# Attention scores on groups of array rows, and the causal mask of the exponentials moved from TensorE to a GpSimd select

## The reference, cut to what matters

```python
# layer 1: 16 heads, each split into two halves of 4 channels (32 half-heads), causal
def _causal_attn(q, k, v, scale, mask):
    s = jnp.einsum('bhqd,bhkd->bhqk', q, k) * scale
    s = jnp.where(mask, s, jnp.finfo(s.dtype).min)
    p = jax.nn.softmax(s, axis=-1)
    return jnp.einsum('bhqk,bhkd->bhqd', p, v)
mask = jnp.tril(jnp.ones((seqlen, seqlen), dtype=bool))[None, None]
a1 = _causal_attn(q1, k1, v1, scale, mask)
a2 = _causal_attn(q2, k2, v2, scale, mask)
y = jnp.concatenate([a1 - lp * a2, a1 + lp * a2], axis=-1)

# layer 2: 16 heads of 8 channels, no mask
scores = jnp.einsum('bhqd,bhkd->bhqk', Q, K) / np.sqrt(Hd).astype(jnp.float32)
attn = jax.nn.softmax(scores, axis=-1)
out = jnp.einsum('bhqk,bhkd->bhqd', attn, V)
```

## Time and profile before

| | kernel before |
|---|---|
| median of 3 runs | 1531.0 us (1527.28 to 1532.28) |
| profiled execution | 1529.98 us |
| its span on the core | 1528.2 us |
| mean granted TensorE clock | 0.899 |
| PE (TensorE matmul) busy | 1342.3 us, 88% of the span |
| PEld (TensorE weight load) busy | 812.0 us, 53% |
| DVE (VectorE) busy | 970.2 us, 63% |
| ACT (ScalarE) busy | 665.5 us, 44% |
| POOL (GpSimd) busy | 203.0 us, 13% |

### The profile page before, as it was taken

One profiled execution on the slowest core, in us unless ns is written; L12 is line 12 of the kernel. 1 busy time (PEld: TensorE's weight loads), 2 busy tenths in 40 slices (PEclk: granted clock), 3 DMA queues, 4 the chain that ended last, 5 costly groups with the idle time before them and its releaser, 6 DMA issues.

```text
span 1528.2 us, 23814 instructions
## 1 busy us (share of the span) xinstructions
PE 1342.3 (88%) x9318; PEld 812.0 (53%) x9334; DVE 970.2 (63%) x2093; ACT 665.5 (44%) x1424; POOL 203.0 (13%) x189
## 2 busy tenths in 40 slices
PE   7977788998897787888989989999779899999999
PEld 4455657876765674343756656654334323234565
DVE  3568743343453677876877876465667888876365
ACT  2444143753541431023433435666446566666621
POOL 1132170000202300035000000044100100000000
PEclk8988698998996987569999999999989999999988
DMA  8000123341000310015253363211212303000000
GB/s 248 6 1 1 29 67 100 98 113 49 27 1 14 70 22 3 0 41 146 89 130 109 107 168 120 92 45 29 64 20 53 64 5 66 3 1 28 1 8 21
DMA packets 65100, 86.22 MB, mean 56 GB/s; under 512 B 9566, under 2 KB 49374, under 8 KB 63326
## 3 DMA queue, kind: packets, MB, share of 16 engines
q1 hardware_dynamic: 60892, 76.30, 19.1%
q0 software_dynamic: 4096, 8.40, 2.0%
HBM read 62.19 MB, written 22.48 MB: 55 GB/s over the span
## 4 chain that ended last, share of the span: by engine, by line
PE 64%; DVE 14%; DMA 8%; ACT 4%; issue 4%; POOL 3%; SPq 2%; DVEq 0%; ACTq 0%
PE psA L404 32%; PE psB L404 25%; PE psB L408 5%; DVE mx L1485 3%; POOL slots_x L1922 2%; PE psA L408 2%; ACT pbuf L1738 2%; DMA wA<-slots_x 2%; POOL tH L1935 1%; DVE st L1168 1%; ACT pbuf L1820 1%; DMA arena<-scr1k 1%; DMA scr1k<-arena 1%; DMA arena<-slots_x 1%; DMA arena<-scr2k 1%
## 5 line engine op out<-in xcount | busy, mean ns | idle before, releaser
L1820 ACT ACTIVATE pbuf<-psA 128x512 f32<-128x512 f32 (+3 forms) x768 | 350.0, 489 | 250.2 <-PE psA L404 243.1
L1485 DVE TENSOR_REDUCE mx<-psA 128x1 f32<-128x512 f32 (+3 forms) x608 | 377.7, 657 | 101.2 <-PE psA L404 97.2
L404 PE MATMUL psA<-arena 64*64 64x128 f32 (+9 forms) x1632 | 243.2, 308 | 14.0 <-DVE mx L1485 11.1
L404 PEld LDWEIGHTS psA<-arena 64*64 64x64 f32 (+3 forms) x1632 | 131.5, 138 | 115.2 <-DVE mx L1485 44.2
L1738 ACT ACTIVATE pbuf<-psA,st,rq 128x128 f32<-128x128 f32 x256 | 92.7, 467 | 112.8 <-DVE st L1172 112.8
L404 PE MATMUL psA<-arena,w 96*128 96x512 bf16 (+4 forms) x320 | 114.8, 411 | 19.3 <-DMA arena<-scr2k 10.4
L404 PE MATMUL psA<-w_identb,w_mdiagT 128*128 128x128 bf16 x512 | 110.9, 243 | 0.0
L404 PE MATMUL psA<-w_mdiagT,w_identb 128*128 128x128 bf16 x512 | 110.0, 223 | 0.0
L404 PE MATMUL psB<-xf,wA 128*128 128x128 f32 x624 | 93.8, 295 | 6.1 <-DMA wA<-in_moe 5.7
L404 PE MATMUL psB<-pbuf,arena 128*5 128x512 f32 (+3 forms) x1024 | 95.3, 445 | 0.4 <-ACT pbuf L1820 0.4
L1935 POOL DMA_INDIRECT tH<-slots_y,slot_i x64 | 62.0, 968 | 237.7 <-DMA slots_y<-tH 219.3
(11 more groups left out here) (295 smaller groups left out, 2136.2 us busy)
## 6 DMA issues: line engine op xcount, KB each, us to landing
wA<-in_moe SPq DMA_DIRECT2D x39, 576.0 KB, 3.8
wA<-in_moe SPq DMA_DIRECT2D x39, 256.0 KB, 3.0
slots_x<-wA SPq DMA_DIRECT2D x20, 256.0 KB, 3.7
slots_y<-tH SPq DMA_DIRECT2D x18, 256.0 KB, 3.6
wA<-slots_x SPq DMA_DIRECT2D x15, 256.0 KB, 4.1
arena<-scr2k SPq DMA_DIRECT2D x48, 64.0 KB
scr1q<-arena SPq DMA_DIRECT2D x4, 384.0 KB, 4.0
scr1k<-arena SPq DMA_DIRECT2D x4, 384.0 KB, 4.1
```

The lines of the kernel that those rows point to most:

```text
L404: return pe.matmul(out, lhsT, rhs, start=start, stop=stop, skip_group_check=True)
L1485: dv.tensor_reduce(m[:, t, h:h + c], topb("mx", lay, b, n)[:, 0:c * k].rearrange("p (c k) -> p c k", c=c), AX.X, ALU.max) \
L1820: ac.activation(pb(lay, b, s, j)[:, 0:T - q0_], scoreb("ex", lay, b, s, j)[:, 0:T - q0_], ACT.Exp, bias=0.0, scale=1.0) \
```

## The change

1. **Row groups.** Each half-head of layer 1 gets its own group of 32 rows (24, with the maxima 27), four groups side by side. Each head of layer 2 gets 64 rows (48, with the maxima 51), two groups. A score matmul reads the rows of its own group alone. Keys are no longer block-diagonal, so `HK` shrinks to a quarter in layer 1 and a half in layer 2. New functions `q_of` and `k_of` give the rows. The maxima passes go through the heads with the row group changing from unit to unit, and `ex` visits the four tiles of a group in the order `HO`.
2. **The mask of `mx`** opens each unit as one matmul over all its diagonal blocks (352 matmuls over 128, 256 or 512 columns in place of 512 over 128), and the scores are added to it.
3. **The mask of `ex`** is gone from TensorE. GpSimd's `affine_select` writes zero above the diagonal into the first 128 columns of four finished tiles at once (128 of them, 128x4x128), and `pv` of layer 1 waits for it (`ex_masked`) in place of the exponential.
4. **The ring `pb`** has twelve tiles in place of eight. The four new ones lie in `arena`.
5. **`pv`, `tail` and the projections** form a stream of their own, `k` in `MERGE`, in place of a fixed place in the main stream. `MERGE` has new contents throughout.
6. **The transfers.** Stacking takes 48 loads of 4 rows per batch in layer 1 (9 of 16, 32 or 48 rows before) and 24 loads of 8 rows in layer 2 (18 of 8 or 16 rows before). The maxima come in by 4 loads in layer 1 and 2 in layer 2 (1 before). The rows of ones are set by a GpSimd memset of the whole of `HK` in place of a transfer from `in_kone`.

The diff, cut to its core:

```diff
 MERGE = (
-    "11ab2ab7c2b2c2bc2bcbcbc3bcb4cb4cb3cb2cbc2b2c2bcbcj4cj2cb2c2jb2j4c3j4cbjcjc2jbjc2j2cb2cjcj2cj8c3j5cjc"
+    "11a3ba3ba9c3bc2bc2bcb4cb2cb2cb2cb5cbcbc2b2cb4cjcj2cjcb3c2j6c2jbjcjcjbc2jcj2cbcj2cj6c2jcjcjb3j4cj2cb2"
...
-        pb = Ring(ptiles)
+        pb = Ring(ptiles + [arena[:, 7680 + T * k:8192 + T * k] for k in range(4)])
+        pfour = [pbuf[:, 2 * k:2 * k + 2, :, 0:P].rearrange("p a b c -> p (a b) c") for k in range(2)]
+        pfour.append(arena[:, 7680:9728].rearrange("p (k c) -> p k c", k=4)[:, :, 0:P])
...
+        HS = {1: 32, 2: 64}
+        HO = {1: (0, 1, 2, 3), 2: (0, 2, 1, 3)}
...
+        def q_of(lay, i, h, rows):
+            p = HS[lay] * (h // 8)
+            return HQ[lay][i][p:p + 6 * HD[lay] + rows, h % 8, :]
...
-                for h, t, o in tops_of(lay)[n]:
-                    k = (t + 1) * P if CAUSAL[lay] else T
-                    m = mm(bank[:, o:o + k], HQ[lay][i][0:96, h % 8, t * P:(t + 1) * P], HK[lay][i][0:96, kof(lay, h), 0:k],
-                           True, not CAUSAL[lay])
-                    if CAUSAL[lay]:
-                        m = mm(bank[:, o + k - P:o + k], mdiagT, identb, False, True)
+                if CAUSAL[lay]:
+                    mm(bank[:, 0:c * k].rearrange("p (c k) -> p c k", c=c)[:, :, k - P:k], mdiagT,
+                       identb.unsqueeze(1).to_broadcast([P, c, P]), True, False)
+                for h, t, o in part:
+                    m = mm(bank[:, o:o + k], q_of(lay, i, h, 0)[:, t * P:(t + 1) * P], k_of(lay, i, h, 0)[:, 0:k], not CAUSAL[lay], True)
...
-                m = mm(bank[:, 0:T - q0_], HK[lay][i][0:HR[lay], kof(lay, g), kb * P:(kb + 1) * P],
-                       HQ[lay][i][0:HR[lay], g % 8, q0_:T], True, not causal)
-                if causal:
-                    m = mm(bank[:, 0:P], identb, mdiagT, False, True)
-                m.then_inc(*ex_mm.up(lay, b, s, j))
+                mm(bank[:, 0:T - q0_], k_of(lay, i, g, 3)[:, kb * P:(kb + 1) * P], q_of(lay, i, g, 3)[:, q0_:T], True, True) \
+                    .then_inc(*ex_mm.up(lay, b, s, j))
...
-                pe.wait_ge(*ex_p.at(lay, b, s, 3))
+                pe.wait_ge(*(ex_masked.at(b, s) if CAUSAL[lay] else ex_p.at(lay, b, s, 3)))
...
+            def ex(lay, b, s, j):
+                if CAUSAL[lay] and j == 3:
+                    v = pfour[pb.turns[lay, b, s, 0] % len(pb.aps) // 4]
+                    po.wait_ge(*ex_p.at(lay, b, s, 3))
+                    po.affine_select(v, v, [[0, 4], [1, P]], ALU.is_ge, fill=0.0, base=0, channel_multiplier=-1).then_inc(*ex_masked.up(b, s))
...
+                for j in range(P // HS[lay]):
+                    r, rows = HS[lay] * j, slice(HS[lay] * j, HS[lay] * j + HS[lay])
+                    for part, n in ((0, 3), (1, 2), (2, 1)):
+                        qs = dr["q"][b][part, rows].rearrange("(i g) c -> i g c", g=8)
                         for k in range(n):
-                            for j in range(2):
...
+                            sy.dma_start(HQ[lay][i][r:r + D], qs).then_inc(*stack_in[b].up(lay))
+                            ks = dr["k"][b][k, rows].rearrange("(i g) c -> i g c", g=8)
+                            if lay == 1:
+                                ks = ks.rearrange("i (h r) c -> i h r c", h=2)[:, :, j, :]
+                            sy.dma_start(HK[lay][i][r:r + D], ks).then_inc(*stack_in[b].up(lay))
+                            r += D
```

More of the change, by code:

```diff
@@ L32 @@
[L32 to L36, removed]
@@ L279, in build, with k_of @@
                      for k, r in (("q", P), ("k", P), ("m", HG[lay]))} for lay in HB}
-        def kof(lay, h):
-            return h % 8 // 4 * 4 + h // 8 if lay == 1 else h
+        def q_of(lay, i, h, rows):
+            p = HS[lay] * (h // 8)
+            return HQ[lay][i][p:p + 6 * HD[lay] + rows, h % 8, :]
+        def k_of(lay, i, h, rows):
+            p = HS[lay] * (h // 8)
+            return HK[lay][i][p:p + 6 * HD[lay] + rows, h % 8 // 4 if lay == 1 else h % 8, :]
         def tile_of(lay, n):
@@ L369, in build @@
         l3_in = signals("weights3_loaded", 1, 16)
-        kone_in = [signals(f"key_ones_loaded{i}", 1, 16) for i in range(NBUF)]
         part_q = [signals(f"q_parts_stored{b}", 1, 16) for b in range(NB)]
@@ L1901, in clr @@
             def clr(lay, b):
-                if lay == 2:
+                if lay == 1:
+                    for t in range(4):
+                        po.wait_ge(*ln_xc.at("h2", t))
+                    po.wait_ge(*bo_done.at(3))
+                    if b:
+                        po.wait_ge(*wo_mm.at(3, 1))
+                        po.wait_ge(*kn_turned.at(3, 3))
+                else:
                     po.wait_ge(*pv_mm.at(1, b + 1, 31))
-                    if b == 0:
-                        po.wait_ge(*pv_mm.at(1, 2, 31))
-                    po.memset(HK[2][b].rearrange("p g c -> p (g c)").bitcast(F32), 0.0).then_inc(*kz_done.up(b))
+                po.memset(HK[lay][b].rearrange("p g c -> p (g c)").bitcast(F32), ONE2).then_inc(*kz_done.up(lay, b))
             def rot(b, n):
@@ L2047, in mxT @@
                 sy.wait_ge(*part_m[b].at(lay))
-                sy.dma_start(HQ[lay][i][96:HR[lay], :, :], dr["m"][b].rearrange("s (j g) c -> (s j) g c", g=8)) \
-                    .then_inc(*max_in[b].up(lay))
+                for j in range(P // HS[lay]):
+                    r = HS[lay] * j + 6 * HD[lay]
+                    sy.dma_start(HQ[lay][i][r:r + 3], dr["m"][b][:, 8 * j:8 * j + 8, :]).then_inc(*max_in[b].up(lay))
             def wi3_():
@@ L2066, in store @@
                     sy.nop()
[L2068 removed]
+            return dict(init=init, xl=xl, wl=wl, st=stored, w2=w2, stack=stack, mxT=mxT, wi3=wi3_, w3=w3, store=store)
         def streams():
@@ L2110, in streams @@
                 main += [("kn0", b, kv) for kv in range(4)] + [("v0", b, j) for j in range(4)] + [("sc", b, i) for i in range(8)]
+            take = []
             for lay in (1, 2):
@@ L2159, in streams @@
                         mix += [("yv", b, i - 1, x)] * (0 < i < 9) + [("tp", b, i, x)] * (i < 8)
-            return [norm, main, ffn, stack, top] + flows + [mix]
+            return [norm, main, ffn, stack, top] + flows + [mix, take]
         def merged():
@@ L2168, in merged @@
                 else:
-                    order += [next(todo["abcdefghij".index(c)]) for _ in range(int(n or 1))]
+                    order += [next(todo["abcdefghijk".index(c)]) for _ in range(int(n or 1))]
                     n = ""
@@ L2265, in constants @@
     c["selq1"], c["selk1"] = c["selq1"].astype(np.float32), c["selk1"].astype(np.float32)
-    one = np.zeros((3, 4, 8, T), np.float32)
-    for h in range(8):
-        one[:, h % 4, h] = 1
-    c["kone1"] = bf(one.reshape(12, 8, T))
-    one = np.zeros((3, 2, 16, T), np.float32)
-    for h in range(16):
-        one[:, h // 8, h] = 1
-    c["kone2"] = bf(one.reshape(6, 16, T))
     c["hsel"] = (i[:, None] // 8 == np.arange(16)[None]).astype(np.float32)
```

133 lines of the change are left out of this document (53 added, 80 removed).

## The result

The changed kernel took 1725.52 us (median of 4 runs, 1719.77 to 1731.78) against 1529.14 us for the kernel before in the same session (4 runs). The ratio is 1.129, with a 95% interval of 1.124 to 1.134. The forecast was 1523 us with a range of 1485 to 1568. It was wrong in size and in sign.

A forecast was written before the change was run, and what follows sets the result against it. TensorE was taken to bound both attentions, taking turns with DVE in the first maxima. Terms +6 +3 -16 -18 +8 +9 = -8 on 1530.0 gave 1522, 1523 as a median, range 1485 to 1568.

The forecast's parts named there:

- Stacks, +8 forecast: Stacked-row loads at batch starts: more, smaller loads change each batch's wait, together +8 us, bounds -24 and +35.
- the second rival: Few-row loads not covered at batch starts: each causal batch starts 9 us late, 35 in place of 8, so 1550; chance 0.22.
- `pv` later and ring of twelve, -18 forecast: Both attentions: later pv ties TensorE and ScalarE less closely, saving a quarter of 78.2 us of waits, bounds 0 and -35.
- the first rival: Later pv gives nothing, as the score waits for its own bank, and the stacks are hidden: 1533; chance 0.20.
- Second attention, -16 forecast: Second attention, 1201 to 1393 us: -40 of overlap, +11 of steps; -16 us taken, bounds -29 and +11.
- First maxima, +6 forecast: First batch's maxima, 588 to 676 us: 88 units at 0.90 us take 79 where they took 73, +6 us.
- the bound that I gave for a gain: First batch's maxima: -12 us if the granted clock rises above 0.55.
- -27 - 32 + 70: Causal attention's TensorE work: -27 us of masks, -32 of overlap, +70 of steps, put at +10; +3 us of time.
- the step of 0.10 us at the full clock: TensorE going from a mask's full tile to a score's smaller tile: 0.096 us a step at 2.4 GHz.
- the overlap of two groups: Scores in different row groups and banks run at once: streaming falls 31 us in layer 1, 41 in layer 2.
- the price of the select between its bounds: GpSimd's select of 128x512: between 0.44 and 1.27 us each, hidden behind ScalarE, so put at 0.
- What all the steps cost together: Neighbours of different tile size go from 526 to 1547: +70 us in the causal attention, +11 in the second.

The follow-up runs named there:

- e10: The changed kernel with every score matmul over the full height of the array in both layers, exponentials' scale 0: 1587.86 us, ratio 1.038 to the kernel before.
- e6: The changed kernel as it is, run again: 1717.71 us, ratio 1.122 to the kernel before.
- e13: The changed kernel with scores over the full height of the array in layer 1 alone: 1608.89 us, ratio 1.052 to the kernel before.
- e14: The changed kernel with scores over the full height of the array in layer 2 alone: 1692.16 us, ratio 1.107 to the kernel before.
- e9: The changed kernel with parts stored in six copies and fewer stack loads, some 15 queue issues a batch in place of 50: 1665.85 us, ratio 1.093.
- e5: The kernel before as it is, run for its trace: 1532.44 us, ratio 1.001.
- e7: The changed kernel with scores over the full height of the array and fewer stack loads together, exponentials' scale 0: 1528.24 us, ratio 0.996 to the kernel before.
- e12: The kernel before with GpSimd's select in place of the exponentials' masks, pv behind the next group's fourth score, ring of eight: 1699.44 us, ratio 1.112.
- e15: The kernel before with the exponentials left unmasked, no select, pv behind the next group's fourth score, ring of eight: 1606.54 us, ratio 1.050.
- e16: The changed kernel without the select, exponentials unmasked, pv waiting for the exponentials themselves: 1722.69 us, ratio 1.122 to the kernel before.
- e8: The changed kernel without the 352 mask matmuls of the maxima: 1677.37 us, ratio 1.094 to the kernel before.

## Why the prediction was wrong, step by step

**The step that failed: every price of the causal and the second attention was taken at the full clock.** The sum read the granted clock of 0.97 and 1.00 off as if it belonged to the stretch. It belonged to the work in it. The prediction counted what the row groups do to columns, overlaps and steps, and for these two stretches had no term, no bound and no rival for what they do to the clock. e10 gives its size. By the prediction's own terms at full clock, going back to full rows would lose 72 us of overlap and save 98 us of steps, 26 us in all. It saved 130, with the clock of the causal stretch going from 0.70 to 0.87. The other 100 us or so are the clock's. That is worked out, not measured by itself, since no kernel had few rows at a high clock over the whole stretch. The rows give a like figure: e6 is busy 606 us at 0.70 in its causal stretch, and the same clocks at 0.87 are 488 us, 118 fewer, of which some would turn into waits. That the low clock comes with few rows is shown by e10, e13 and e14, each against e6, and that it does not come with the waits by e9. Against the steps around the masks speak the stretches from 1280 us (no mask, 0.70) and from 950 us (masks close together, 1.00) in the section on the result.

The number of rows does not settle the level by itself. In the first maxima the kernel before also runs at the low level, with scores over 96 rows, and so does the changed kernel while TensorE is busy 99% of the time. With 120 rows, in e10, it has 0.80. From 605 to 650 us, for the kernel before, the changed one and e10:

```profile
605.00:650.00 45.00, 39.74 (x175) 14.12 (x174) 36.98 (x61) 0.00 (x0) 0.00 (x0) 0.50 0.00 0
605.00:650.00 45.00, 44.56 (x145) 12.97 (x145) 35.73 (x56) 0.00 (x0) 0.00 (x0) 0.50 0.00 0
605.00:650.00 45.00, 37.64 (x195) 17.07 (x193) 40.81 (x75) 0.15 (x1) 1.02 (x1) 0.80 0.01 3
```

What holds the kernel before at the low level here was not tested.

**Stacks, +8 forecast.** The mechanism was the second rival's and its size was off. The rival's 35 us were for rows that come late. e9 puts the transfers at 45 to 52 us. The prediction took 0.335 us for an issue, from a group of loads of layer 2, where the same rows have 1.53 / 3 = 0.51 us for the loads of layer 1, and it asked only who waits for the stack. It missed that a pair takes 1.15 us, and that the weights of the experts are queued behind 27.6 us of it. Of the 78.4 us of waits, 42.2 are theirs.

**`pv` later and ring of twelve, -18 forecast.** Nothing of it is seen. The weight load's waits for ScalarE in e5 and in e7, 580 to 1460 us:

```profile
PEld psA L404 <- ACT pbuf L1820: 117.3, 230, 1.0
```

```profile
PEld psA L412 <- ACT pbuf L1827: 80.3, 161, 1.7
...
PEld psA L412 <- ACT arena L1827: 43.2, 83, 1.0
```

117.3 against 80.3 + 43.2 = 123.5 us, as the first rival said. Its reason, that the score waits for its own bank, fits but was not tested. The ring and the order are not without effect, though: with eight tiles, in the order of before, the select cost 93 us (e12, e15), with twelve in the new order nothing (e16). That the changed kernel is only slower and so has time for the select is not the reason, for in e7, as fast as the kernel before, TensorE waits 3.5 us for it in all. Ring and order were not tested apart. The saved masks then show up to a small part only: e7 is 3 us under the kernel before, where 27 us of masks had gone.

**Second attention, -16 forecast.** It came out at +5, and at 0 in e6. Without the overlap it takes 191 us at a clock of 0.98 (e14), and with it 192 at 0.89 (e6), so what the overlap gives the lower clock takes back.

**First maxima, +6 forecast.** They took 82.9 us against 88.2, -5. The clock stayed at 0.54, so it was not the bound that I gave for a gain. With full rows it was 73 us at 0.74 (e10), and without masks 70 at 0.56 (e8). These 13 us are what the 16,384 columns of this batch's masks take at 1.2 GHz (13.7 us), so no cost of their 174 steps is seen beside it, where the prediction took 176 x 0.14 = 25 us. Why the maxima came out shorter than before was not tested.

**A slip in the sum.** -27 - 32 + 70 is +11 and not +10. It changes nothing.

**Right were** the step of 0.10 us at the full clock, the overlap of two groups, the price of the select between its bounds, and that it is hidden. What all the steps cost together was not: e8 took out some 700 of them with their 27 us of columns, 97 us by the prediction's prices, and gained 40.

## What to carry to other kernels

A granted clock in a profile belongs to the work in that stretch. A change that makes each matmul use less of the array has to be priced at 1.2 GHz too, and the sum compared at both levels before anything else. Here the stretches where products over 128 rows stood between the scores kept the full clock. Small tiles that overlap save columns, and here lost more by the clock than they saved. Splitting a transfer costs the queue for every piece, and the price is paid by whatever is queued behind it. A mask moved to another engine stands in that engine's queue: the same select cost 93 us with a ring of eight tiles, and nothing measurable with twelve and a new order.

## What the runs showed of the hardware that I had not expected

- TensorE 91% busy, mainly with scores of 24 and 27 rows, their masks and their products with the values, ran at a granted clock of 0.52 for 100 us. With the experts' products over 128 rows between such scores it had 1.00 for 50 us. The same order over the full height ran its whole stretch at 0.87 to 0.91.
- The second attention, with scores over 48 and 51 rows and products on 128 rows, had 0.87 to 0.90, against 0.98 to 1.00 with scores over 96 to 115 rows.
- The rows of zeros in the keys of the kernel before do not stand in the way of the full clock: three of four half-heads' rows are zero in each key, and it has 1.00 from 1120 to 1160 us.
- Two loads of four rows each hold SyncE's queue for 1.15 us, while three loads of sixteen took 1.53.
- One of the chips ran the kernel before in 1645 us in place of 1530, at a mean granted clock of about 0.865 in place of 0.90. No trace of that kernel was taken there.
